# Attention and expert tail on one core: band bias by products for 32 keys in column groups over 96 stacked rows, prologue loads in another order, gathers six tiles ahead and scatters three behind

## The chip, the core and the metric

The program runs on one NeuronCore of one Trainium2 chip. A core has five engines with a queue of instructions each: TensorE (PE, with its weight loads as PEld), VectorE (DVE), ScalarE (ACT), GpSimd (POOL) and SyncE (SP, which here only issues DMAs). The metric is the device time of one execution in microseconds (us). The kernel before took 760.58 us, the median of three runs (757.05 to 767.64).

## What is computed

Two layers act on x, which is (2, 1024, 128) in f32. The attention of the first is what the change touches most.

```python
x = x + attention(layernorm(x), Wq, bq, Wk, bk, Wv, bv, rel_bias)   # 16 heads, head size 8, S = 1024
x = x + channel_mix(layernorm(x), W_r, W_k, W_v, mu_r, mu_k)        # sigmoid(.) * (relu(.)^2 @ W_v.T)
x = x + spiral_conv_block(layernorm(x), ..., w1, b1, w2, b2)        # long convolution, norm, 128 -> 512 -> 128
x = x + experts(layernorm(x), gate_w, w1, w3, w2)                   # 2048 tokens, top 2 of 8, hidden 352

# attention
scores = einsum('bqhd,bkhd->bhqk', q, k) / sqrt(8)
n = maximum(query - key, 0)          # distance; 0 for keys later than the query
bias = rel_bias[bucket(n)]           # 32 buckets: n itself below 16, logarithmic above, the last from 31 on
attn = softmax(scores + bias, axis=-1)
context = einsum('bhqk,bkhd->bqhd', attn, v)

# experts
for e in range(8):
    out = (silu(xe @ w1[e].T) * (xe @ w3[e].T)) @ w2[e].T            # only rows routed to e count
```

For a head the bias depends on query - key alone. It has one value for all keys later than the query, another for all keys 31 or more before it, and varies only between: in a tile of 128 keys, for at most 160 queries.

## The kernel before, in words

**Prologue.** Sixteen row tiles of x are normed by DVE. In four chunks of 512 tokens, PE transposes the normed rows (`transposes(c)`, L497) and projects them to q, k and v (`project(c)`, L513, L514, L516). Q and k are split into three bf16 parts each (by ACT and DVE for chunks 0 and 1, POOL takes part for chunks 2 and 3), which SP writes to DRAM (`parts_out`, L278, L280). A small table of bias values per distance goes to DRAM too, in f32 and in three bf16 parts (L266, L268).

**Pairs.** The scores are computed for 16 pairs of heads of one batch each (`Pair`). A pair's operands are loaded from DRAM into one of three sets, `set` = pair modulo 3: queries and a row of bias steps (`load_queries`, L289 and L291), keys (`load_keys`, L219) and the band tables in f32 and in bf16 parts (`load_tables`, L296 and L301). Row r of a table holds the bias values from an offset r on, and a product with a reversing matrix (FLIPB) puts the rows at the keys they belong to. A pair has 20 loads; they all count on one semaphore, `ops_in`. PE waits for the whole of it before a pair's first product. SP issues them in this order two pairs ahead, once PE has used up the last pair that had the set (`b_ready`). Pair 0's keys are loaded on ACT's queue.

**A tile.** Each pair is 16 tiles j, head a = j % 2 and key block kb = j // 2 of 128 keys. For a tile PE does, in this order: two products 128 x 512 of the transposed scores (`scores_T`, L552, into `psB`), between them two of the untransposed scores for the row maxima (`scores`, L541, into one of three `psA` banks), which belong to a tile six ahead (`AHEAD`) and thus, at the end of a pair, to the next pair; the band bias added to `psB` (`band_T`, L563: one product for each bf16 part, 128 x 160, 128 x 128 in the last key block, and in key block 3, where the band crosses a bank's border at column 512, a product for each side); and then values of an earlier tile (`values`, L580: eight products, 32 output partitions each, in four column groups, `tile_position=(0, g)`). ACT turns `psB` into probabilities (L468, L470). DVE reduces the `psA` banks to row maxima (L700, L705, L706), reduces those at the end of a pair (L712), and PE transposes them once in a pair (`max_transpose`, L591, at tile 12). They go through DRAM into rows of the next pair's queries (SP L308, L312). A product of `scores` waits for its bank to be freed by DVE (`free_bank`), one of `scores_T` for ACT's exponential two tiles before.

The scores of pair 0 and of six tiles of pair 1 come first (a loop of 22 steps at the end of the prologue, scores only), with the chunks 2 and 3 between them. POOL's queue has the splits for chunks 2 and 3, the addition of v's bias, and behind these the loads of the later layers' weights (L398).

**Tail.** The other layers run in chunks behind the attention. The experts come last: the rows are sorted by expert into 46 tiles of 128 (`TILES`). POOL gathers a tile's rows by an indirect DMA (L944) four tiles ahead into a ring of 8 (`RING_X`); PE transposes them, multiplies by w1 and w3 (L1167) and w2 (L1190); DVE puts the result into a ring of 4 (`RING_Y`, L1434), and POOL scatters it by an indirect DMA (L950) two tiles behind.

## Time and profile before

| | |
|---|---|
| median of three runs | 760.58 us (757.05 to 767.64) |
| profiled execution | 759.78 us, its span 758.0 us |
| mean granted TensorE clock | 0.907 |
| PE busy | 623.5 us (82%) |
| DVE busy | 509.1 us (67%) |
| ACT busy | 428.8 us (57%) |
| POOL busy | 164.1 us (22%) |

The span runs from the first to the last instruction of the profiled execution. Busy time is that in which an engine has an instruction in work. PE's matmuls are pipelined, so their durations overlap and a busy PE is not one at its peak. PEclk is the clock that was granted to TensorE, 1.00 for 2.4 GHz and 0.50 for 1.2 GHz. SPq is SP's own sequencer as it issues DMAs. An engine's shares are means over stages that differ: prologue up to about 75 us, pairs to 465 us, then the other layers, and the expert tiles from 589 to 745 us.

### The profile page before, as it was taken

To read this page: it belongs to the slowest core of one execution; us is meant where nothing else is said; L and a number is where in the kernel's file an instruction comes from. 1 tells how busy PE (TensorE), PEld (TensorE's weight loads), DVE (VectorE), ACT (ScalarE), POOL (GpSimd) and SP (SyncE) were. 2 spreads that over 40 slices of the span, in tenths; PEclk is the share of its full clock that TensorE was granted. 3 is DMA by queue.
4 is the path that set the end of the run, shared out by engine and by line. 5 is a ranking of instruction groups with operands and counts; after the bars stand their busy time and mean duration, and the time that the engine had idled before them with its cause. 6 is when DMAs were issued, how large, how long until landed. Compare 5 with 4: busy or idle time off the path is not lost. (4 is left out here: it accounts for less than half of the span.)

```text
span 758.0 us, 14698 instructions
## 1 busy us (share of the span) xinstructions
PE 623.5 (82%) x5140; PEld 292.4 (39%) x5140; DVE 509.1 (67%) x1627; ACT 428.8 (57%) x769; POOL 164.1 (22%) x199
## 2 busy tenths in 40 slices
...
...
DMA packets 62842, 40.17 MB, mean 53 GB/s; under 512 B 36462, under 2 KB 54759, under 8 KB 62477
## 3 DMA queue, kind: packets, MB, share of 16 engines
...
q8 instruction: 42, 0.69, 0.4%
...
q14 instruction: 30, 0.25, 0.1%
...
## 5 line engine op out<-in xcount | busy, mean ns | idle before, releaser
L468 ACT ACTIVATE sb_probs<-psB 128x128 f32<-128x128 f32 (+7 forms) x256 | 167.2, 653 | 92.2 <-PE psB L563 92.0
L700 DVE TENSOR_REDUCE sb_max_parts<-psA 128x1 f32<-128x512 f32 x256 | 176.5, 690 | 50.7 <-PE psA L541 43.0
L541 PE MATMUL psA<-sb_k_operand,sb_q_operand 53*128 53x512 bf16 x512 | 170.2, 403 | 35.2 <-DMA sb_bias_table_parts<-bias_parts 26.7
L580 PE MATMUL psV<-sb_probs,sb_v_operand 128*32 128x256 f32 x2048 | 160.7, 392 | 0.1
L552 PE MATMUL psB<-sb_q_operand,sb_k_operand 53*128 53x512 bf16 x512 | 157.1, 387 | 0.1
L470 ACT ACTIVATE sb_probs<-psB,sb_far_bias 128x896 f32<-128x896 f32 (+6 forms) x224 | 153.7, 686 | 0.0
L705 DVE TENSOR_REDUCE sb_max_parts<-psA 128x1 f32<-128x352 f32 (+1 forms) x256 | 133.0, 519 | 0.1
L563 PE MATMUL psB<-sb_bias_table_parts,sb_flip_b 128*128 128x160 bf16 (+2 forms) x864 | 98.4, 228 | 0.0
L563 PEld LDWEIGHTS psB<-sb_bias_table_parts,sb_flip_b 128*128 128x128 bf16 x864 | 50.9, 98 | 102.2 <-issue 102.2
L374 POOL COPY sb_v_operand<-sb_v_by_pair 128x64 f32<-128x64 f32 x32 | 7.2, 257 | 340.1 <-PE psB L563 328.7
L706 DVE CUSTOM_DVE_ANT_0 sb_band_scores<-psA,sb_bias_tables 128x160 f32<-128x160 f32 (+1 forms) x256 | 79.6, 311 | 0.0
L1167 PE MATMUL bank<-wt_w,context_T 128*128 x184 | 69.4, 500 | 6.5 <-DVE t_hm L1428 3.3
L552 PEld LDWEIGHTS psB<-sb_q_operand,sb_k_operand 53*128 53x128 bf16 x512 | 28.8, 94 | 99.3 <-issue 89.9
L950 POOL DMA_INDIRECT rows_y<-t_ys,t_place x46 | 46.5, 1011 | 58.7 <-DVE t_ys L1434 47.4
L541 PEld LDWEIGHTS psA<-sb_k_operand,sb_q_operand 53*128 53x128 bf16 x512 | 33.5, 94 | 64.3 <-DVE sb_max_parts L700 21.8
L1044 ACT ACTIVATE t_su<-bank 128x352 f32<-128x352 f32 x46 | 21.3, 464 | 65.2 <-PE bank L1167 40.5
L1428 DVE TENSOR_TENSOR t_hm<-t_su,bank 128x352 f32<-128x352 f32 x46 | 24.0, 521 | 47.8 <-PE bank L1167 32.0
L580 PEld LDWEIGHTS psV<-sb_probs,sb_v_operand 128*32 128x32 f32 x2048 | 42.2, 108 | 30.8 <-ACT sb_probs L468 0.6
L1048 ACT COPY context_T<-bank 128x512 f32<-128x512 f32 (+2 forms) x49 | 27.4, 558 | 44.3 <-issue 15.6
L1434 DVE COPY t_ys<-bank 128x128 f32<-128x128 f32 x46 | 13.4, 291 | 54.5 <-remote 32.2
L1190 PE MATMUL bank<-wt_w,context_T 128*128 (+1 forms) x276 | 40.1, 281 | 11.0 <-DVE t_ys L1434 10.9
L944 POOL DMA_INDIRECT t_xs<-rows_x,t_token x46 | 44.8, 973 | 13.9 <-issue 13.6
...
## 6 DMA issues: line engine op xcount, KB each, us to landing
...
```

Source lines behind the costliest of these rows:

```text
L468: ins = nc.scalar.activation(out[:, 0:edge], scores[:, 0:edge], ACT.Exp)
L470: ins = nc.scalar.activation(out[:, edge:S], scores[:, edge:S], ACT.Exp, bias=DELTA[:, bass.ds(p.n * 2 + a, 1)])
L541: nc.tensor.matmul(PA[slot % 3][:], QO[64 * a:64 * a + ROWS, p.set, 128 * qb:128 * qb + 128], KO[64 * a:64 * a + ROWS, p.set, at:at + 512] ...
L552: nc.tensor.matmul(PB[:, 1024 * a + lo:1024 * a + lo + 512], KO[64 * a:64 * a + ROWS, p.set, 128 * kb:128 * kb + 128], QO[64 * a:64 * a + ...
L563: ins = nc.tensor.matmul(PB[:, 1024 * a + c0:1024 * a + c1], FLIPB[:], TP[:, p.set, a, part, c0 - 128 * kb:c1 - 128 * kb], start=False, st ...
L580: ins = nc.tensor.matmul(PV[g:g + 32, at:at + 256], VB[:, p.set, a, kb, :], P[:, kb % KB_BUFS, a, half * 512 + at:half * 512 + at + 256], ...
L700: nc.vector.tensor_reduce(mx[:, 0:1], score_bank(t, 0)[:], AX.X, ALU.max).then_inc(s["a_used"], 1)
L705: nc.vector.tensor_reduce(mx[:, 1:2], ps[:, 0:352 + edge], AX.X, ALU.max)
L706: nc.vector.tensor_tensor_reduce(SC[:, t % 2, edge:160], ps[:, 352 + edge:512], reversed_table(p, a, edge, 160), 1.0, -3.0e38, ALU.add, AL ...
L944: pool.indirect_dma_start(XS[:, n % RING_X, :], None, XMD[h], bass.IndirectOffsetOnAxis(TOK[h][:, k:k + 1], 0)).then_inc(x_in[n % RING_X], 16)
L950: pool.indirect_dma_start(YD[h], bass.IndirectOffsetOnAxis(PLACE[h][:, k:k + 1], 0), YS[:, n % RING_Y, :], None, bounds_check=2 * S - 1, o ...
L1167: nc.tensor.matmul(out[:, 0:HID], HX[:, (n - 2) % 3, 384:512], t[w][:, bass.ds(experts[n], 1), :].rearrange("d o h -> d (o h)"), start=Tru ...
```

## The change

It has three parts.

**The band.** `band_T` treats each 32 keys of a tile apart. The three bf16 parts of the table are stacked as 3 x 32 = 96 rows, and the stationary matrix `FLIP3` (96 rows) holds the reversing 32 x 32 block three times, so that one product adds up the three parts. Group i of 32 keys needs the queries from 32 i on: 128, 96, 64 and 32 columns (64 for the last, where the band reaches into the next key block), and goes into its own column group. In key block 3 a fifth product serves the columns behind the bank's border for the last group. The table `TP` becomes 96 x 192 per head and is loaded by three DMAs for each head instead of two for both; `LOADS` becomes 24.

**The prologue.** SP issues pair 0's tables ahead of the q and k parts, the bias steps by a function of their own (`load_steps`), and the keys of head 1; ACT issues those of head 0, at its third chunk. PE takes chunk 2 ahead of the first scores, and the fourth chunk's q, k and v projections are put at three steps of the scores' loop instead of one.

**The experts.** Gathers run six tiles ahead, scatters three behind, and `RING_Y` is 5; in a step the scatter stands ahead of the gather.

```diff
     REL, SEL = sb("rel", [NB, 2 * H]), sb("sel", [NB, WCOLS])
-    FLIP, FLIPB, IDB = sb("flip", [128, 128]), sb("flip_b", [128, 128], BF16), sb("ident_b", [128, 128], BF16)
+    FLIP, FLIP3, IDB = sb("flip", [128, 128]), sb("flip_3", [96, 128], BF16), sb("ident_b", [128, 128], BF16)
     KRB = sb("key_rows_b", [5, 2 * S], BF16)
...
     QO, KO = sb("q_operand", [128, 3, S], BF16), sb("k_operand", [128, 3, 2 * S], BF16)
-    TT, TP = sb("bias_tables", [128, 3, 2, 160]), sb("bias_table_parts", [128, 3, 2, 3, 160], BF16)
+    TT, TP = sb("bias_tables", [128, 3, 2, 160]), sb("bias_table_parts", [96, 3, 2, 192], BF16)
     VB = sb("v_operand", [128, 3, 2, NBLK, 32])
...
              "b_ready exp_done pv_done evac_done max_parts max_psum max_rows max_out max_in "
-             "bq_scaled m_step own_v").split()
+             "bq_scaled m_step own_v flip_zero").split()
     s = {n: sem(n) for n in names}
...
     ops_in = [sem(f"ops_in{n}") for n in range(3)]
-    LOADS = 2 * (3 + 4 + 1) + 4
+    LOADS = 2 * (3 + 4 + 1) + 2 + 6
...
-    def load_keys(eng, p):
-
-        for a in range(2):
+    def load_keys(eng, p, heads=range(2)):
+
+        for a in heads:
             at = p.n * (16 * 3 * S) + a * DH * 3 * S
...
                                  ).then_inc(ops_in[p.set], 16)
+
+        def load_steps(p):
+            for a in range(2):
                 sp.dma_start(QO[64 * a + ROW_STEP:64 * a + ROWS, p.set, :],
...
                              ).then_inc(ops_in[p.set], 16)
-            parts = TP[:, p.set, :, :, :].rearrange("p h a c -> p (h a) c")
-            for at, seg, n in ((0, DIAG, 128), (128, EDGE, 32)):
-                sp.dma_start(parts[:, :, at:at + n], bass.AP(WPD.tensor, p.n * (2 * 3 * NPARTS) + seg,
-                                                             [[1, 128], [NPARTS, 6], [1, n]])
-                             ).then_inc(ops_in[p.set], 16)
+            for a in range(2):
+                for at, seg, n in ((0, DIAG + 96, 128), (128, DIAG + 96, 32), (160, EDGE, 32)):
+                    sp.dma_start(TP[:, p.set, a, at:at + n],
+                                 bass.AP(WPD.tensor, (p.n * 2 + a) * (3 * NPARTS) + seg, [[NPARTS, 3], [1, 32], [1, n]])
+                                 ).then_inc(ops_in[p.set], 16)
...
-        parts_out(0)
-        parts_out(1)
         sp.wait_ge(s["w_out"], 16)
         sp.wait_ge(s["wp_out"], 16)
+        load_tables(Pair(0, 0))
+        parts_out(0)
         sp.wait_ge(s["steps_out"], 16)
+        load_steps(Pair(0, 0))
+        parts_out(1)
         for c in range(2):
...
         load_queries(Pair(0, 0))
-        load_tables(Pair(0, 0))
         for c in range(2):
             sp.wait_ge(k_out[c], 32)
+        load_keys(sp, Pair(0, 0), heads=(1,))
         load_queries(Pair(0, 1))
+        load_steps(Pair(0, 1))
         load_keys(sp, Pair(0, 1))
...
                 load_queries(p + 2)
+                load_steps(p + 2)
                 load_keys(sp, p + 2)
...
         pool.memset(MHALF[:], -0.5).then_inc(s["half_ready"], 1)
+        pool.memset(FLIP3[:], 0.0).then_inc(s["flip_zero"], 1)
         pool.memset(STEPS[:, 3:5, :], 0.0).then_inc(s["steps_ready"], 1)
...
             nc.scalar.copy(XT[:, 512 * c:512 * c + 512], PV[:]).then_inc(s["xt_ready"], 1)
+            if c == 2:
+                for n in range(2):
+                    act.wait_ge(k_out[n], 32)
+                load_keys(act, Pair(0, 0), heads=(0,))
             act.wait_ge(s["bq_scaled"], 1)
...
                            V_BANKS[c].rearrange("p (n m c) -> p n m c", n=4, m=8)).then_inc(s["v_read"], 1)
-            if c == 1:
-                for n in range(2):
-                    act.wait_ge(k_out[n], 32)
-                load_keys(act, Pair(0, 0))
-
         def max_copy(p):
...
-        def project(c):
+        def project(c, what="qkv"):
             pe.wait_ge(s["xt_ready"], c + 1)
...
             xt = XT[:, 512 * c:512 * c + 512]
-            nc.tensor.matmul(Q_BANKS[c], WQ[:], xt, start=True, stop=True).then_inc(s["q_psum"], 1)
-            nc.tensor.matmul(K_BANKS[c], WK[:], xt, start=True, stop=True).then_inc(s["k_psum"], 1)
-            for n in range(4):
-                ins = nc.tensor.matmul(V_BANKS[c][:, 128 * n:128 * n + 128], xt[:, 128 * n:128 * n + 128], WV[:],
-                                       start=True, stop=True)
-            ins.then_inc(s["v_psum"], 1)
+            if "q" in what:
+                nc.tensor.matmul(Q_BANKS[c], WQ[:], xt, start=True, stop=True).then_inc(s["q_psum"], 1)
+            if "k" in what:
+                nc.tensor.matmul(K_BANKS[c], WK[:], xt, start=True, stop=True).then_inc(s["k_psum"], 1)
+            if "v" in what:
+                for n in range(4):
+                    ins = nc.tensor.matmul(V_BANKS[c][:, 128 * n:128 * n + 128], xt[:, 128 * n:128 * n + 128], WV[:],
+                                           start=True, stop=True)
+                ins.then_inc(s["v_psum"], 1)
...
         def band_T(p, j):
+
+
+
             kb, a = j // 2, j % 2
-            for half in range(2):
-                lo = half * 512
-                c0, c1 = max(lo, 128 * kb), min(lo + 512, 128 * kb + 160)
-                if c0 < c1:
-                    for part in range(3):
-                        ins = nc.tensor.matmul(PB[:, 1024 * a + c0:1024 * a + c1], FLIPB[:],
-                                               TP[:, p.set, a, part, c0 - 128 * kb:c1 - 128 * kb],
-                                               start=False, stop=part == 2)
+            edge = kb not in (3, 7)
+            for i in range(4):
+                at, n = 1024 * a + 128 * kb + 32 * i, 128 - 32 * i
+                table = TP[:, p.set, a, 0:n]
+                if i == 3 and edge:
+                    n, table = 64, TP[:, p.set, a, 128:192]
+                ins = nc.tensor.matmul(PB[32 * i:32 * i + 32, at:at + n], FLIP3[:, 96:128], table,
+                                       start=False, stop=True, tile_position=(0, 32 * i))
+            if kb == 3:
+                ins = nc.tensor.matmul(PB[:, 1024 * a + 512:1024 * a + 544], FLIP3[:], TP[:, p.set, a, 160:192],
+                                       start=False, stop=True)
             ins.then_inc(s["b_ready"], 1)
...
-        for c in range(2):
+        for c in range(3):
             transposes(c)
             project(c)
-        pe.wait_ge(s["flip_ready"], 2)
+        pe.wait_ge(s["flip_ready"], 4)
         pe.wait_ge(s["key_copies"], 32)
...
             turn, j = (Pair(0, -2), t + 16 - AHEAD) if t < AHEAD else (Pair(0, -1), t - AHEAD)
-            if t in (2, 8):
-                transposes(2 + t // 8)
-            if t in (5, 11):
-                project(2 + t // 8)
+            if t == 3:
+                transposes(3)
+            if t in (6, 8, 10):
+                project(3, "qkv"[t // 2 - 3])
             if t == AHEAD + MAX_AT:
...
         dve.wait_ge(s["flip_in"], 32)
-        nc.vector.tensor_copy(FLIPB[:], FLIP[:]).then_inc(s["flip_ready"], 1)
+        dve.wait_ge(s["flip_zero"], 1)
+        for n in range(3):
+            at = 32 * n
+            nc.vector.tensor_copy(FLIP3[at:at + 32, 96:128], FLIP[at:at + 32, 96 - at:128 - at]
+                                  ).then_inc(s["flip_ready"], 1)
         dve.wait_ge(s["w_in"], 16 * 6)
...
 TILES_FROM = START[1] + AT["gates"] + 5
-SLOTS = TILES_FROM + TILES + 4
+SLOTS = TILES_FROM + TILES + 5
 TABLE = 3 * SLOT_TILES
-RING_X, RING_Y = 8, 4
+RING_X, RING_Y = 8, 5
+GATHERED, SCATTERED = 6, 3
...
         n = slot - TILES_FROM - 2
-        return [n] if -2 <= n < TILES + 2 else []
+        return [n] if -2 <= n < TILES + 3 else []
...
             for n in tile_at_slot(slot):
+                if 0 <= n - SCATTERED < TILES:
+                    scatter(n - SCATTERED)
                 if n == -2:
-                    for m in range(3):
+                    for m in range(GATHERED - 1):
                         gather(m)
-                elif n + 4 < TILES:
-                    gather(n + 4)
-                if n >= 2:
-                    scatter(n - 2)
+                elif n + GATHERED < TILES:
+                    gather(n + GATHERED)
...
                                      ).then_inc(s[done], 1)
-            if n > -2:
+            if -2 < n <= TILES + 1:
                 pe.wait_ge(s["hx"], n + 2)
...
                 ins.then_inc(s["hx_psum"], 1)
-            if n >= 2:
+            if 2 <= n < TILES + 2:
                 y = n - 2
...
                 V.tensor_tensor(HM[:, n % 2, 0:HID], SU[:, n % 2, :], V_PS[:, 0:HID], ALU.mult).then_inc(s["hm"], 1)
-            if n >= 2:
+            if 2 <= n < TILES + 2:
                 y = n - 2
```

PE's queue in a middle tile of a pair, before. L552 is `scores_T`, L541 `scores`, L563 the band, L580 the values.

```order
L552 MATMUL psB<-sb_q_operand,sb_k_operand 128x512
L541 MATMUL psA<-sb_k_operand,sb_q_operand 128x512
L552 MATMUL psB<-sb_q_operand,sb_k_operand 128x512
L541 MATMUL psA<-sb_k_operand,sb_q_operand 128x512
L563 MATMUL psB<-sb_bias_table_parts,sb_flip_b 128x160 x3
L580 MATMUL psV<-sb_probs,sb_v_operand 32x256 x4
```

The same place after the change. L562 is `scores_T`, L551 `scores`, L577 the band, L596 the values.

```order
L562 MATMUL psB<-sb_q_operand,sb_k_operand 128x512
L551 MATMUL psA<-sb_k_operand,sb_q_operand 128x512
L562 MATMUL psB<-sb_q_operand,sb_k_operand 128x512
L551 MATMUL psA<-sb_k_operand,sb_q_operand 128x512
L577 MATMUL psB<-sb_bias_table_parts,sb_flip 32x128
L577 MATMUL psB<-sb_bias_table_parts,sb_flip 32x96
L577 MATMUL psB<-sb_bias_table_parts,sb_flip 32x64 x2
L596 MATMUL psV<-sb_probs,sb_v_operand 32x256 x4
```

Only the band's rows differ; its four products stand between the scores and the values, which have 32 output partitions as well.

PE's queue in the prologue, behind the second chunk, before. L497 are transposes, L513, L514 and L516 the projections to q, k and v.

```order
L541 MATMUL psA<-sb_k_operand,sb_q_operand 128x512 x4
L497 MATMUL psV<-sb_ident,xn 128x128 x4
L541 MATMUL psA<-sb_k_operand,sb_q_operand 128x512 x6
L513 MATMUL psB<-xn_T,sb_wq 128x512
L514 MATMUL psB<-xn_T,sb_wk 128x512
L516 MATMUL psB<-sb_wv,xn_T 128x128 x4
L541 MATMUL psA<-sb_k_operand,sb_q_operand 128x512 x6
L497 MATMUL psV<-sb_ident,xn 128x128 x4
L541 MATMUL psA<-sb_k_operand,sb_q_operand 128x512 x6
L513 MATMUL psB<-xn_T,sb_wq 128x512
L514 MATMUL psB<-xn_T,sb_wk 128x512
L516 MATMUL psB<-sb_wv,xn_T 128x128 x4
```

After the change (L504 transposes; L521, L523, L526 the projections):

```order
L504 MATMUL psV<-sb_ident,xn 128x128 x4
L521 MATMUL psB<-xn_T,sb_wq 128x512
L523 MATMUL psB<-xn_T,sb_wk 128x512
L526 MATMUL psB<-sb_wv,xn_T 128x128 x4
L551 MATMUL psA<-sb_k_operand,sb_q_operand 128x512 x6
L504 MATMUL psV<-sb_ident,xn 128x128 x4
L551 MATMUL psA<-sb_k_operand,sb_q_operand 128x512 x6
L521 MATMUL psB<-xn_T,sb_wq 128x512
L551 MATMUL psA<-sb_k_operand,sb_q_operand 128x512 x4
L523 MATMUL psB<-xn_T,sb_wk 128x512
L551 MATMUL psA<-sb_k_operand,sb_q_operand 128x512 x4
L526 MATMUL psB<-sb_wv,xn_T 128x128 x4
```

The third chunk stands ahead of all scores, the fourth is in three pieces with scores between them.

SP's queue where it has written the steps, up to the second chunk's parts, before:

```order
L270 DMA step_rows<-sb_steps 32x5120
L278 DMA q_parts<-sb_q_split 128x512
L280 DMA q_parts<-sb_q_split 128x2x512
L278 DMA k_parts<-sb_k_split 128x512
L280 DMA k_parts<-sb_k_split 128x2x512
```

After the change:

```order
L270 DMA step_rows<-sb_steps 32x5120
L299 DMA sb_bias_tables<-bias_vectors 128x2x128
L299 DMA sb_bias_tables<-bias_vectors 128x2x32
L304 DMA sb_bias_table_parts<-bias_parts 96x1x128
L304 DMA sb_bias_table_parts<-bias_parts 96x1x32 x2
L304 DMA sb_bias_table_parts<-bias_parts 96x1x128
L304 DMA sb_bias_table_parts<-bias_parts 96x1x32 x2
L278 DMA q_parts<-sb_q_split 128x512
L280 DMA q_parts<-sb_q_split 128x2x512
```

Pair 0's tables, which stood behind its queries, are now issued first, and by eight DMAs instead of four.

## Rows read from the trace of the kernel before

**Rows 1.** The page's costliest groups: line, engine, tiles | busy us, mean ns | idle before

```profile
L580 PE MATMUL psV<-sb_probs,sb_v_operand 128*32 128x256 f32 x2048 | 160.7, 392 | 0.1
```

**Rows 2.** Three windows of 20 us: busy time per engine, then PEclk, DMA share

```profile
60.00:80.00 20.00, 15.38 (x45) 3.33 (x44) 19.72 (x57) 3.11 (x7) 19.86 (x28) 0.52 0.30 67
...
240.00:260.00 20.00, 19.90 (x211) 6.74 (x208) 18.94 (x58) 16.09 (x28) 0.41 (x2) 1.00 0.18 40
...
440.00:460.00 20.00, 20.00 (x195) 6.75 (x197) 0.00 (x0) 16.50 (x28) 0.00 (x0) 1.00 0.02 5
```

**Rows 3.** Timeline, one tile on PE: start us, us, engine, line, tiles

```profile
251.28 0.39 PE L552 MATMUL psB<-sb_q_operand,sb_k_operand 53*128 53x512 bf16 x1
...
251.81 0.34 PE L563 MATMUL psB<-sb_bias_table_parts,sb_flip_b 128*128 128x128 bf16 x3
...
252.08 0.64 PE L580 MATMUL psV<-sb_probs,sb_v_operand 128*32 128x256 f32 x8
...
252.66 0.39 PE L552 MATMUL psB<-sb_q_operand,sb_k_operand 53*128 53x512 bf16 x1
```

**Rows 4.** Timeline, the maxima's product on PE, behind the values of a tile

```profile
271.01 0.64 PE L580 MATMUL psV<-sb_probs,sb_v_operand 128*32 128x256 f32 x8
...
271.47 0.22 PE L591 MATMUL psA<-sb_ident_b,sb_max_high_low 128*32 128x128 bf16 x1
...
271.62 0.39 PE L552 MATMUL psB<-sb_q_operand,sb_k_operand 53*128 53x512 bf16 x1
```

**Rows 5.** Timeline, DVE, at the change from one pair to the next

```profile
245.36 0.20 DVE L712 TENSOR_REDUCE sb_row_max<-sb_max_parts 128x16 f32<-128x48 f32 x1
...
268.68 0.20 DVE L712 TENSOR_REDUCE sb_row_max<-sb_max_parts 128x16 f32<-128x48 f32 x1
...
269.64 0.68 DVE L700 TENSOR_REDUCE sb_max_parts<-psA 128x1 f32<-128x512 f32 x1
...
270.91 0.69 DVE L700 TENSOR_REDUCE sb_max_parts<-psA 128x1 f32<-128x512 f32 x1
```

**Rows 6.** Timeline, the prologue: norms, last load, first scores, projection, DVE's wait

```profile
24.49 2.14 DVE L657 TENSOR_SCALAR xn<-x,sb_ln_mv,sb_ln_rstd 128x128 f32<-128x128 f32 x8
...
30.59 1.06 SPq L301 DMA_DIRECT2D sb_bias_table_parts<-bias_parts  x2
...
35.16 1.01 PE L541 MATMUL psA<-sb_k_operand,sb_q_operand 53*128 53x512 bf16 x3 [13.94 <-DMA sb_bias_table_parts<-bias_parts]
...
41.38 2.08 PE L513 MATMUL psB<-xn_T,sb_wq 128*128 128x512 f32 x2
...
47.44 0.69 DVE L700 TENSOR_REDUCE sb_max_parts<-psA 128x1 f32<-128x512 f32 x1 [4.71 <-PE psA L541]
```

**Rows 7.** Timeline, weight loads on POOL, pair 2's table load, its first product

```profile
67.80 0.79 POOL L398 DMA_DIRECT2D wt_r<-in_W_r  x1
...
84.41 13.09 SPq L301 DMA_DIRECT2D sb_bias_table_parts<-bias_parts  x2
...
103.28 0.61 PE L541 MATMUL psA<-sb_k_operand,sb_q_operand 53*128 53x512 bf16 x1 [12.77 <-DMA sb_bias_table_parts<-bias_parts]
```

**Rows 8.** Timeline, SP's queue, first and last load of one pair's operands

```profile
253.56 1.81 SPq L289 DMA_DIRECT2D sb_q_operand<-q_parts  x3
...
261.64 1.06 SPq L301 DMA_DIRECT2D sb_bias_table_parts<-bias_parts  x2
```

**Rows 9.** Timeline, the expert stage: two tiles on PE and on POOL

```profile
649.57 1.45 PE L1167 MATMUL bank<-wt_w,context_T 128*128 x4 [0.27 <-issue]
...
651.96 1.35 PE L1167 MATMUL bank<-wt_w,context_T 128*128 x4
...
650.25 0.98 POOL L944 DMA_INDIRECT t_xs<-rows_x,t_token  x1 [0.30 <-issue]
...
652.85 0.97 POOL L944 DMA_INDIRECT t_xs<-rows_x,t_token  x1 [0.30 <-issue]
```

**Rows 10.** Waits of the whole span: who for whom, us in total, times, longest

```profile
DVE t_ys L1434 <- remote: 32.2, 9, 3.8
```

## The prediction, made before the changed kernel ran

> **What bounds the kernel now.** I read the page first, then the busy time by windows, then the timeline of one tile, one change of pairs, the prologue and the expert stage, and last the waits. The attention covers about 75 to 465 us of the 758 us. In its middle PE is busy 19.9 of 20 us, DVE 18.9 and ACT 16.1, at clock 1.00; behind 440 us, where DVE has nothing left, PE is at 20.00 of 20 [rows 2]. So PE sets the pace, and DVE stands close behind. How close is seen in two places. A tile takes PE 1.38 us with a 128-column band (about 1.42 with 160 columns): 0.53 for the score products, 0.27 for the three band products, 0.58 for the values [rows 3]. DVE, where it has a backlog, needs 1.27 us for the same tile, and 0.96 us between pairs for the row maximum [rows 5]. A pair takes 23.3 us now [rows 5]; DVE's own floor is 16 x 1.27 + 1.0 = 21.3.
>
> Before that lie two long waits for operand loads: 13.9 us ahead of the first scores [rows 6], and 12.8 us at 90.5 us, where PE waits for pair 2's operands while the expert weights fill the DMA engines [rows 7]. Two projections inside the first pair's scores also starve DVE, one of them for 4.71 us [rows 6].
>
> **The band products.** Three products with 128 output partitions become four with 32 each, in four column groups, over 96 rows instead of 128; two tiles in 16 get a fifth. Do column groups run at once? The values say so: 8 products of a mean of 392 ns [rows 1] are done in 0.64 us [rows 3]. A second thing can be read there. Behind a tile's values, the score product starts 0.58 us after they began [rows 3], but the maxima's product, which also has 32 columns, starts 0.46 us after [rows 4]. A change of shape thus costs about 0.1 us, and none is paid between two 32-column shapes. The new band has the values' shape, so one of three changes per tile goes as well. Band and change fall from 0.27 (0.31 at 160 columns) to about 0.06: PE's tile becomes 0.53 + 0.06 + 0.58 = 1.17 us.
>
> The bounds: if the four products ran one behind another and the change stayed, the phase would be 352/384 of the present one, since their widths sum to 128 + 96 + 64 + 64 columns against 384 in [rows 3]: 0.25 us, and a tile 1.36. Below, nothing can take more than the whole 0.31. I take 1.17, by [rows 3, 4]. For short products the Trainium skill (TensorEngine Tiling (Array Packing), Instruction Overhead) says that each matmul carries some 60 cycles whatever its width. Four of these would be 0.1 us instead of 0.06 and the last tiles of the stage would cost 1 us more; the middle would not change, since DVE sets it either way.
>
> At 1.17 PE passes DVE, and a pair takes DVE's 21.3, not 16 x 1.17. I add 0.3 for the tile with two pieces of values and the tile in which ACT also copies the context out: 21.6, a gain of 1.7 us. DVE works on 14 pairs behind the wait at 103 us: **-24 us** (-12 with a tile of 1.36, -28 at the bare floor). The ten tiles ahead of that wait gain 0.14 each: **-1.4**. Behind DVE's last pair some 22 tiles remain; there PE's 1.17 and ACT's 16.5 of 20 us [rows 2], which is 1.17 of 1.42, are level. With 1.20 per tile: **-4.8** (-1 to -5.5).
>
> **The operand loads.** The band tables now are 6 DMAs per pair instead of 2: four more on SP's queue, and nothing is taken off it. Two issues take 1.06 us [rows 8], so about 2.1 us is added to a queue that is busy for 9.1 us from the start of a pair (253.56 to 262.70). DVE turns to that pair at 269.64 [rows 5], 16.1 us after the first issue, and the product has to be there 0.6 earlier: 15.5. The ten tiles between shrink by 1.4. The margin from last issue to need thus goes from 6.4 to 2.9 us. The flight of the last load is at most 31.65 to 35.16 = 3.5 us, as the prologue shows with 1536 small pieces under way [rows 6]. The new tables have 576 pieces (96 rows, three segments, two heads), so I take the flight below 2.9 and the cost as **0**; up to 0.6 us for 13 pairs, 8 us, is in the range.
>
> **The prologue.** Pair 0's tables are issued ahead of the q and k parts, one head's keys move from ACT's queue to SP's, and behind the q parts SP has ten issues left instead of twelve. The last issue comes at about 31.2 instead of 31.65, with 16 rows in place of 1536 pieces; the load should be there at 33. Into the wait goes the third projection block. Its norms are done by 26.6 [rows 6]; transposes, copy and three projections of about 2 us each (L513 takes 2.08 at the half clock [rows 6]) end at about 33.4. The scores start there: **-1.6** (0 to -3). DVE's 4.71 us for this block goes. The fourth block is cut in three, each of 2 us less the 0.7 us of scores that stand ready; that about equals what it costs in one piece: together **-4.9** (-2 to -7).
>
> **The wait for pair 2.** The weight loads start at 67.80, and the wait ends at 103.28, 35.5 us later; SP's two table issues alone were held up 13.09 us [rows 7]. In the new order the weights start about 13 us earlier, at 55 (the fourth block's keys are ready earlier, and POOL's split and addition follow). 960 of the 1536 pieces that came last are gone, for which I take 3 us. Pair 2's operands would be there at 55 + 32.5 = 87.5. PE reaches them 15.3 us after pair 0's start, now 90.5, then about 90.5 - 1.6 - 4.9 - 1.4 = 82.6. The wait shrinks to 5: **-7.5** (0 to -12.8).
>
> **The expert stage.** Gathers run six tiles ahead instead of four, scatters three behind instead of two, with a ring of five. PE's short tile is 2.39 us, POOL's pair of transfers 2.60 [rows 9], yet the stage averages about 3.2. Its long waits are DVE's on something that the profile calls remote, nine times, up to 3.8 us [rows 10]. Nothing there names a late gather or scatter, so I only count the few late gathers: **-3**. If the remote waits come from the two-deep scatters, POOL's 2.60 is the new pace, 0.6 x 37 tiles = -22; if deeper gathers crowd POOL, +5.
>
> **The sum.** -24 - 1.4 - 4.8 + 0 - 1.6 - 4.9 - 7.5 - 3 = -47. The profiled execution took 759.8, which gives 712.6; the median shown is 0.8 above it: **713 us**.
>
> **The rivals.** First, the column groups don't overlap and PE stays the bound at 1.36: the middle gains 12 instead of 24, the end 1 instead of 4.8: 713 + 12 + 4 = 729. Against it stand [rows 4]; for it, that no row shows 96-row products there. Chance 0.15. Second, the operands land later than I take it, and the wait for pair 2 stays: 713 + 8 + 7.5 = 729. Chance 0.13. Third, the remote waits go: 713 - 19 = 694, chance 0.10. Fourth, the change leaves the path alone, because PE's records only look full: within 2%, about 750; [rows 2] speak against it, 0.04.
>
> The one on the other side is TensorE's clock. Once DVE sets the pace, PE stops for a moment in every tile. That is the state of 60 to 80 us, where DVE is busy 19.7 of 20 and the granted clock is 0.52, nearly its 1.2 GHz level [rows 2]. At that level a tile of 1.17 takes 2.34. It decides from 3.4 us of loss per pair, which eats the 47 us over 14 pairs: three or four tiles of each 16 at the low level. If half of them were, 8 x 1.07 = 8.6 us per pair would be added: 713 + 120 = 833. Against it: a slow PE is the bound again, and so gets no pauses; and in the stretch of 60 to 80 PE did a third of the work per tile. Chance 0.05. The Trainium skill (TensorE: Matmul & The Clock Gate, A second HAM failure mode) describes such a case, where small pauses between groups of products let the clock swing between its two levels.
>
> **How the numbers follow.** My forecast, 704 to 722, has 0.53. The range for 8 in 10 takes in the first two rivals and half of the third: 699 to 734. A measurement of this kernel can tell some 2% from no change, which is 745 to 776. Faster by more: 0.53 + 0.15 + 0.13 + 0.10, less a little for sums of bad ends, 0.89; same 0.06; slower 0.05.
>
> **What would show it.** Right: band products in one burst under 0.3 us with the values right behind; DVE without gaps at 1.27 us per tile, pairs of 21.3 to 21.9; PE's score products released by DVE; the first wait about 12 us with projections in it, the second about 5. Wrong: pairs above 22.5; a wait of every pair's first product for a table DMA; a clock below 1.00 between 110 and 420 us; expert tiles off 3.2 us.

## The result: faster by 4.8%, 13 us above the forecast

| | before | changed |
|---|---|---|
| median | 759.74 us of 4 runs (757.05 to 767.64) | 726.11 us of 4 runs (721.22 to 730.41) |
| ratio | | 0.9518 (0.9466 to 0.957) |
| profiled execution | 759.78, span 758.0 | 725.86, span 724.0 |

The forecast was 713 with a range of 699 to 734. The page of the changed kernel begins:

```profile
span 724.0 us, 15152 instructions
## 1 busy us (share of the span) xinstructions
PE 585.4 (81%) x5332; PEld 267.5 (37%) x5332; DVE 497.6 (69%) x1629; ACT 426.8 (59%) x769; POOL 164.5 (23%) x200
```

The same windows as [rows 2], the last one moved to where DVE's work ends (busy time of each engine, then granted clock, DMA share, GB/s):

```profile
60.00:80.00 20.00, 13.19 (x39) 2.55 (x38) 15.59 (x50) 2.00 (x5) 17.16 (x29) 0.50 0.57 188
240.00:260.00 20.00, 18.69 (x237) 5.77 (x239) 19.42 (x63) 16.75 (x29) 0.41 (x2) 1.00 0.19 46
400.00:420.00 20.00, 19.48 (x245) 5.46 (x237) 3.77 (x14) 19.07 (x34) 0.00 (x0) 1.00 0.03 6
```

In the middle PE no longer fills its time and DVE does; behind DVE's last pair PE and ACT are level. One tile on PE and the change of pairs on DVE, the counterparts of [rows 3] and [rows 5]:

```profile
162.78 0.39 PE L562 MATMUL psB<-sb_q_operand,sb_k_operand 53*128 53x512 bf16 x1
...
163.32 0.23 PE L577 MATMUL psB<-sb_bias_table_parts,sb_flip 96*32 96x128 bf16 x4
163.37 0.62 PE L596 MATMUL psV<-sb_probs,sb_v_operand 128*32 128x256 f32 x8
163.92 0.39 PE L562 MATMUL psB<-sb_q_operand,sb_k_operand 53*128 53x512 bf16 x1
```

```profile
143.24 0.20 DVE L732 TENSOR_REDUCE sb_row_max<-sb_max_parts 128x16 f32<-128x48 f32 x1
...
164.75 0.20 DVE L732 TENSOR_REDUCE sb_row_max<-sb_max_parts 128x16 f32<-128x48 f32 x1
...
165.36 0.68 DVE L720 TENSOR_REDUCE sb_max_parts<-psA 128x1 f32<-128x512 f32 x1
```

The four band products last 0.23 us together, and the values follow 0.05 us behind their start. A tile takes PE 1.14 us where nothing holds it, against 1.38 to 1.42. A pair takes 21.51 us (164.75 less 143.24) against 23.32.

Where the 34.0 us of span went, read from the first score reduction on DVE of each pair (for the last pair also that of its last tile, where the tiles behind DVE's last begin) and the last product of the transposed scores:

| stretch | before | changed | difference | forecast |
|---|---|---|---|---|
| start to DVE's pair 0 | 35.85 | 39.08 | +3.2 | -1.6 |
| pair 0's scores | 32.16 | 26.29 | -5.9 | -4.9 |
| pair 1's, with the wait for pair 2 | 35.99 | 34.03 | -2.0 | -8.9 |
| 14 pairs on DVE | 327.3 | 302.5 | -24.8 | -24 |
| the tiles behind DVE's last | 30.8 | 25.7 | -5.1 | -4.8 |
| tail | 295.9 | 296.4 | +0.5 | -3 |

The middle came as forecast. The prologue gave 4.7 where 15.4 was expected. Its rows, first SP's and the first scores, then POOL's weights, SP's tables of pair 2 and PE's two waits (start, duration, then in brackets the idle time before and what ended it):

```profile
20.19 4.42 SPq L304 DMA_DIRECT2D sb_bias_table_parts<-bias_parts  x6
...
30.45 3.72 SPq L289 DMA_DIRECT2D sb_q_operand<-q_parts  x6
...
34.27 1.34 SPq L219 DMA_DIRECT2D sb_k_operand<-k_parts  x4
...
38.39 1.01 PE L551 MATMUL psA<-sb_k_operand,sb_q_operand 53*128 53x512 bf16 x3 [4.96 <-DMA sb_k_operand<-k_parts]
...
61.41 0.79 POOL L406 DMA_DIRECT2D wt_r<-in_W_r  x1
...
76.93 0.58 PE L562 MATMUL psB<-sb_q_operand,sb_k_operand 53*128 53x512 bf16 x1 [4.86 <-DMA sb_q_operand<-row_maxima]
...
81.34 15.88 SPq L304 DMA_DIRECT2D sb_bias_table_parts<-bias_parts  x6
...
98.69 0.61 PE L551 MATMUL psA<-sb_k_operand,sb_q_operand 53*128 53x512 bf16 x1 [6.43 <-DMA sb_bias_table_parts<-bias_parts]
```

The last key load of pair 0 is issued by 35.61 (34.27 + 1.34), and PE starts 2.8 us later. Not all of the +3.2 belongs to the change. PE's first transposes, before and changed, already lie 1.3 us apart, since DVE's second norm waited 1.65 us for x instead of 0.34, and nothing of the change stands ahead of that load:

```profile
10.35 1.12 PE L497 MATMUL psV<-sb_ident,xn 128*128 128x128 f32 x4 [2.14 <-DVE xn L657]
```

```profile
11.69 1.12 PE L504 MATMUL psV<-sb_ident,xn 128*128 128x128 f32 x4 [3.19 <-DVE xn L673]
```

This start varies from 10.4 to 12.1 us over the profiles below. From the first transposes to the first scores it is 24.8 us before and 26.7 changed (26.7 to 27.0 in all eight profiles with this order and these loads on SP): +1.9 us is the change's. The wait for pair 2's tables shrank from 12.77 [rows 7] to 6.43, but a new one of 4.86 stands ahead of it, for pair 0's maxima, whose small transfers lie among the weights.

### The profile page after: what moved, and what is told of

It reads as the page before. It is cut to its first block and busy times, and to the rows that moved or that the text cites. A ratio compares the mean times of both kernels' runs of the same rounds, so it can differ in the third digit from the quotient of the medians.

```text
span 724.0 us, 15152 instructions
## 1 busy us (share of the span) xinstructions
PE 585.4 (81%) x5332; PEld 267.5 (37%) x5332; DVE 497.6 (69%) x1629; ACT 426.8 (59%) x769; POOL 164.5 (23%) x200
## 5 line engine op out<-in xcount | busy, mean ns | idle before, releaser
L551 PE MATMUL psA<-sb_k_operand,sb_q_operand 53*128 53x512 bf16 x512 | 181.4, 411 | 26.2 <-DMA sb_bias_table_parts<-bias_parts 11.4
L562 PE MATMUL psB<-sb_q_operand,sb_k_operand 53*128 53x512 bf16 x512 | 161.1, 389 | 7.1 <-DMA sb_q_operand<-row_maxima 6.0
L596 PE MATMUL psV<-sb_probs,sb_v_operand 128*32 128x256 f32 x2048 | 157.7, 387 | 0.3 <-ACT sb_probs L475 0.3
L562 PEld LDWEIGHTS psB<-sb_q_operand,sb_k_operand 53*128 53x128 bf16 x512 | 31.5, 94 | 105.8 <-issue 51.1
L551 PEld LDWEIGHTS psA<-sb_k_operand,sb_q_operand 53*128 53x128 bf16 x512 | 39.6, 94 | 82.4 <-DVE sb_max_parts L720 41.8
L577 PE MATMUL psB<-sb_bias_table_parts,sb_flip 96*32 96x64 bf16 (+3 forms) x1024 | 59.3, 214 | 0.0
L577 PEld LDWEIGHTS psB<-sb_bias_table_parts,sb_flip 96*32 96x32 bf16 x1024 | 26.3, 93 | 87.9 <-issue 87.9
L1065 ACT ACTIVATE t_su<-bank 128x352 f32<-128x352 f32 x46 | 21.4, 466 | 62.7 <-PE bank L1188 38.4
L596 PEld LDWEIGHTS psV<-sb_probs,sb_v_operand 128*32 128x32 f32 x2048 | 44.5, 110 | 5.0 <-ACT sb_probs L475 0.8
```

The source lines that it names most:

```text
L551: nc.tensor.matmul(PA[slot % 3][:], QO[64 * a:64 * a + ROWS, p.set, 128 * qb:128 * qb + 128], KO[64 * a:64 * a + ROWS, p.set, at:at + 512] ...
L562: nc.tensor.matmul(PB[:, 1024 * a + lo:1024 * a + lo + 512], KO[64 * a:64 * a + ROWS, p.set, 128 * kb:128 * kb + 128], QO[64 * a:64 * a + ...
L577: ins = nc.tensor.matmul(PB[32 * i:32 * i + 32, at:at + n], FLIP3[:, 96:128], table, start=False, stop=True, tile_position=(0, 32 * i))
L596: ins = nc.tensor.matmul(PV[g:g + 32, at:at + 256], VB[:, p.set, a, kb, :], P[:, kb % KB_BUFS, a, half * 512 + at:half * 512 + at + 256], ...
```

## The experiments

The column "before" is the median of the kernel before on the same chip, and the ratio is against it. The kernel before itself took 738 to 765 us, by the chip, so the ratios are compared, and stretches of the profiles. Three more kernels leave something out and were run once each, beside a kernel before of 761.89 or 764.96; they stand in the text.

| kernel | median | before | ratio (interval) | last scores product at |
|---|---|---|---|---|
| changed | 726.11 | 759.74 | 0.9518 (0.9466 to 0.957) | 427.6 |
| tables on POOL | 723.54 | 761.89 | 0.9498 (0.9451 to 0.9545) | 425.1 |
| weights spread | 715.08 | 761.89 | 0.9404 (0.9342 to 0.9465) | 416.6 |
| prologue undone | 735.56 | 761.89 | 0.9691 (0.9622 to 0.9761) | 436.8 |
| both | 711.30 | 764.96 | 0.9329 (0.925 to 0.9407) | 412.2 |
| experts undone, scatter first | 739.55 | 764.96 | 0.9682 (0.9594 to 0.9769) | 430.7 |
| experts as before | 704.43 | 744.17 | 0.9476 (0.9428 to 0.9525) | 428.2 |
| gather first | 695.07 | 744.17 | 0.9345 (0.9293 to 0.9396) | 428.5 |
| band only | 716.30 | 744.17 | 0.9646 (0.9596 to 0.9695) | 436.8 |
| best | 681.27 | 738.41 | 0.9214 (0.9165 to 0.9263) | 414.0 |

### Who sets a pair: DVE's first reduction reads a quarter

```diff
-nc.vector.tensor_reduce(mx[:, 0:1], score_bank(t, 0)[:], AX.X, ALU.max)
+nc.vector.tensor_reduce(mx[:, 0:1], score_bank(t, 0)[:, 0:128], AX.X, ALU.max)
```

> The first reduction of each tile on DVE reads 128 of its 512 columns (0.69 us becomes about 0.28), so three quarters of the keys of that half are left out of the row maxima; everything else as changed. Theory A (DVE sets the pair time): pairs fall from 21.52 to the next bound, which is PE with 16 tiles of 1.13 to 1.39 us and its hiccups, or SP's issues, 19 to 20.5 us; 14 pairs give 14 to 35 us, about 700 us in all. Rival B (SP's load loop sets it: 14.0 us to the first product): the pair is 14.0 plus six tiles of 1.13, 20.8 us, and each first product waits for its table load by over 0.5 us. Rival C (PE or ACT sets it): pairs stay at 21.3 to 21.5.

One run: 718.26 us. Change of pairs on DVE, a pair's first product on PE, and two windows:

```profile
140.20 0.20 DVE L732 TENSOR_REDUCE sb_row_max<-sb_max_parts 128x16 f32<-128x48 f32 x1
160.81 0.20 DVE L732 TENSOR_REDUCE sb_row_max<-sb_max_parts 128x16 f32<-128x48 f32 x1
```

```profile
161.57 0.39 PE L551 MATMUL psA<-sb_k_operand,sb_q_operand 53*128 53x512 bf16 x1 [0.76 <-DMA sb_bias_table_parts<-bias_parts]
...
204.11 0.39 PE L551 MATMUL psA<-sb_k_operand,sb_q_operand 53*128 53x512 bf16 x1 [2.10 <-DMA sb_bias_table_parts<-bias_parts]
```

```profile
140.00:160.00 20.00, 18.72 (x255) 5.43 (x258) 16.53 (x66) 17.93 (x32) 0.41 (x2) 1.00 0.20 49
...
204.00:208.00 4.00, 3.89 (x34) 0.96 (x36) 2.11 (x8) 2.00 (x4) 0.00 (x0) 0.57 0.06 11
```

With DVE at 16.5 of 20 us a pair falls from 21.51 to 20.61, and no further: now every first product waits for its tables. So DVE sets the pair in the changed kernel, and the table loads, which come last on SP's queue, stand 0.9 us behind it. That is both theories at once, A for the kernel as it is and B for the next step. The gain in total, 7.8 us, is less than A's low end, since B's bound was so near and some pairs took 21.9 to 22.9. One of those is in the rows: PE stood still for 2.10 us ahead of 204.11, and from 204 to 208 the granted clock is 0.57, near the 1.2 GHz level; from 208 on it is back at 1.00.

### The tables issued by POOL

```diff
-                load_tables(p + 2)                    # SP
+                load_tables(pool, p + 2)              # POOL, behind values(p + 1)
```

Pair 0's and 1's tables stand in POOL's queue where it waits in the prologue, pair 2's ahead of the weights; they count on semaphores of their own.

> All eight table loads of a pair are issued on POOL's queue instead of SP's, in the prologue too; everything else as changed. Theory A (DVE sets the pair time of 21.52 us; the six-fold issues on SP only cost where they run late): SP's issues of a pair fall from 12.5 to about 7.2 us, the small waits of a pair's first product for a table load vanish, the two long pairs (21.89 and 22.79) become 21.5, and the other pairs stay at 21.4 to 21.5; in the prologue the first scores come at about 34 instead of 38.4. In total 3 to 6 us less than the changed kernel: 720 to 723. Rival B (the loop of SP's queue sets the pair time: 14.0 us from a pair's first issue to its first product and 7.5 to the next issue): pairs fall below 21.1, and the total to 712 or less. Rival C (the order of SP's prologue costs nothing, the first scores wait for the third projection block): they stay at 38.

Median 723.54, ratio 0.9498: inside the changed kernel's interval. SP's issues of a pair, first in the changed kernel and then here, and the one long wait that PE has here:

```profile
129.00 3.71 SPq L289 DMA_DIRECT2D sb_q_operand<-q_parts  x6
...
136.18 0.90 SPq L299 DMA_DIRECT2D sb_bias_tables<-bias_vectors  x2
137.12 4.38 SPq L304 DMA_DIRECT2D sb_bias_table_parts<-bias_parts  x6
```

```profile
149.57 3.65 SPq L301 DMA_DIRECT2D sb_q_operand<-q_parts  x6
...
153.98 2.70 SPq L220 DMA_DIRECT2D sb_k_operand<-k_parts  x8
```

```profile
105.09 0.60 PE L566 MATMUL psB<-sb_q_operand,sb_k_operand 53*128 53x512 bf16 x1 [10.81 <-DMA sb_q_operand<-row_maxima]
```

SP's issues fall from 12.5 us to 7.1, and pairs stay at 21.52: B has fallen. The long pairs of the changed kernel (21.89, 22.79) are gone, which with two smaller ones is worth 1.5 us. The first scores come at 36.4, 2.0 earlier, not 4.4; and 1.3 of the 2.0 is the earlier arrival of x. From the first transposes to the first scores it is 25.95 us instead of 26.71. PE waits for the key load there, so C's reason is wrong, but its size (nothing) is nearer than A's: the keys still wait behind six query loads. Pair 2's scores begin 12 us earlier, at 86.7, and then PE waits 10.8 us for pair 1's maxima. The wait has moved, not gone: it belongs to whatever small transfer comes while the weights are under way.

### The weights in pieces

```diff
-        for dst, src in later_loads:
-            pool.dma_start(dst, src).then_inc(loaded, 16)
...
+            if 1 <= p.n <= 12:
+                for dst, src in later_loads[p.n - 1::12]:
+                    pool.dma_start(dst, src).then_inc(loaded, 16)
```

w1 and w3 are cut by expert, w2 by two experts.

> The loads of the later layers' weights are cut into pieces of one or two experts and issued by POOL in pairs 1 to 12, four a pair, instead of in one go at 61 us; everything else as changed. Theory A (the weight traffic makes both remaining waits of the prologue, 4.86 us for pair 0's maxima and 6.43 us for pair 2's tables): both vanish, pair 2's first product comes at about 87 instead of 98.7, and the pairs behind stay at 21.5: 11 us less, about 715. Rival B (the loads are late through SP's own queue, 5.4 us of table issues): the waits shrink by less than half, 721 or more. Rival C (the traffic is only moved: each pair's own loads, which land 1.5 us ahead of need, now come late by the pieces' time): pairs of 22.0 and more, no gain in total, 724 to 728.

Median 715.08, ratio 0.9404. Pair 2's first product, and that of pair 11:

```profile
86.95 0.39 PE L551 MATMUL psA<-sb_k_operand,sb_q_operand 53*128 53x512 bf16 x1
```

```profile
282.27 0.39 PE L551 MATMUL psA<-sb_k_operand,sb_q_operand 53*128 53x512 bf16 x1 [0.87 <-DMA sb_bias_table_parts<-bias_parts]
```

Both waits are gone, as A has it: 86.95 without a wait, at the full clock. Of the 11.7 us against the changed kernel 0.9 is the earlier arrival of x. The edit cuts the loads and also spreads them over twelve pairs; which of the two does it was not separated. C is there too but small: four pairs take 22.2 to 22.6 (the next expectation says six), 3 us in all more than at 21.52. That the pieces delay their loads is likely, not shown: the changed kernel has long pairs too.

### Both

> Weights spread over pairs 1 to 12 and all table loads on POOL's queue. Theory A (DVE sets the pairs, the two prologue waits are the weights' and the long pairs come from SP's late issues): first scores at 36.4, pair 0's maxima without a wait, pair 2's first product at 86, every pair 21.5 without the 22.2 to 22.6 that six pairs show with the weights spread alone: 3 to 5 us less than its 715, 710 to 712. Rival B (the pieces sit ahead of the tables in POOL's queue and make them late): pairs of 22.5 and more, 716 or above.

Median 711.30, ratio 0.9329, as A has it. Pair 2 starts at 85.0, and all pairs but two take 21.52 (21.8 and 22.1).

### The prologue's order undone

The order on SP, PE and ACT is that of before; band and expert stage are the changed ones.

```diff
-        for c in range(3):
+        for c in range(2):
             transposes(c)
...
-            if t == 3:
-                transposes(3)
-            if t in (6, 8, 10):
-                project(3, "qkv"[t // 2 - 3])
+            if t in (2, 8):
+                transposes(2 + t // 8)
+            if t in (5, 11):
+                project(2 + t // 8)
```

> The changed kernel with the prologue's order of before on PE, SP and ACT (third and fourth projection blocks in the scores' loop, tables behind the queries, pair 0's keys on ACT), with the new band and the new expert stage. Theory A (the new order cost 3.2 us at the first scores and gave 5.9 back in the projections, and the rest was lost in the wait for the weights): the first scores come at about 38 (35.2 plus 2 to 3 for four more table issues), pair 0's scores take 32 us instead of 26, and pair 2's first product comes at 103 to 106 instead of 98.7: 4 to 7 us more than the changed kernel, 730 to 733. Rival B (the order is worth nothing): 726 within 2.

Median 735.56, ratio 0.9691. First scores 38.2, pair 0's scores 31.6 us, pair 2's first product 106.5, the last scores product 9.2 us later than in the changed kernel: A, a little above its range. Undoing the order brings the first scores no earlier than 38.2 (26.5 us behind the first transposes), since the four more table issues then stand ahead of them in their old place. So the +1.9 at the start comes with the band's part, not with the new order; the kernel with the band alone, below, has the same 26.7. How much of it is the issues themselves is open: with all tables on POOL only 0.8 came back.

### The band alone, and without its products

Band only: prologue and expert stage as before.

> Only the band's part of the change (products for 32 keys in column groups, 96 stacked rows, six table loads a pair), with the prologue's order and the expert stage of before. Theory A (the band alone gives the 23 us of 13 pairs, about 2 us at the first pair, and 5 in the last 22 tiles, and the four more issues of SP cost 3 us at the first scores): the last band product at 436, which is 26 earlier than before, and 732 to 737 in all. Rival B (the band and the new prologue only work together): a gain below 20 us, over 740.

Ratio 0.9646; 716.30 us against 744.17 on that chip, and 25.3 us earlier than before at the last scores product (436.8 against 462.1, the latter from a profile on which the kernel before took 759.78). A's times for the whole were meant for a chip on which the kernel before takes 760. On the same chip the kernel with the new prologue as well (experts as before) takes 704.43: the prologue adds 11.9, of which the profiles show 8.6 by the last scores product.

```diff
-                band_T(p, j)
+                # b_ready comes from the second product of scores_T
```

> The band products are left out (the bias of near keys is missing); the second product of the transposed scores releases ACT in their place. Looked at where DVE has nothing left, some 20 tiles ahead of the last band, in which PE's tile is 1.13 us with the band and was 1.38 to 1.42 before. Theory A (the four products run at once and cost 0.05 to 0.06, and their change of shape is shared with the values): PE's tile falls by at most 0.06, to 1.07 to 1.10, or is set by ACT's 1.13 to 1.17 and does not fall at all; pairs in the middle stay at 21.4 to 21.5. Rival B (the products still cost 0.15 to 0.2 a tile): 0.95 in tiles where ACT doesn't hold PE, and pairs fall by over 1 us.

One run: 720.6 us. One tile behind DVE's last pair, without the band and (second fence) in the changed kernel:

```profile
402.90 0.60 PE L562 MATMUL psB<-sb_q_operand,sb_k_operand 53*128 53x512 bf16 x2
...
403.43 0.64 PE L598 MATMUL psV<-sb_probs,sb_v_operand 128*32 128x256 f32 x8
```

```profile
405.87 0.60 PE L562 MATMUL psB<-sb_q_operand,sb_k_operand 53*128 53x512 bf16 x2
...
406.41 0.23 PE L577 MATMUL psB<-sb_bias_table_parts,sb_flip 96*32 96x128 bf16 x4
...
406.45 0.62 PE L596 MATMUL psV<-sb_probs,sb_v_operand 128*32 128x256 f32 x8
```

The values start 0.53 us after the tile's start without the band and 0.58 with it: the four products cost 0.05. Tiles take 1.10 there and 1.13 in the changed kernel, but ACT is busy nearly all the time in both (17.74 of 18 us and 19.07 of 20), so the 0.05 is read on PE alone. Pairs take 21.29 instead of 21.52. B has fallen.

The fifth product of key block 3 is another matter. It has 128 output partitions, not 32:

```profile
416.69 0.60 PE L562 MATMUL psB<-sb_q_operand,sb_k_operand 53*128 53x512 bf16 x2
...
417.38 0.19 PE L580 MATMUL psB<-sb_bias_table_parts,sb_flip 96*128 96x32 bf16 x1
417.50 0.64 PE L596 MATMUL psV<-sb_probs,sb_v_operand 128*32 128x256 f32 x8
```

There the values start 0.81 us after the tile's start, so this one product of 32 columns costs 0.23, over four times as much as the other four together, and its tiles take 1.39 us instead of 1.13. The prediction put it at nothing. It stands between 32-partition products and so adds changes of shape, which agrees with the 0.1 us for each that the prediction read from [rows 3, 4], though no run changes its shape alone. In the middle it is hidden behind DVE.

### The expert stage

Only eight tiles gathered:

```diff
-                elif n + GATHERED < TILES:
+                elif n + GATHERED < RING_X:
```

> In the expert stage only the first 8 tiles are gathered, and the others work on what lies in the ring, so that POOL issues one indirect DMA for a tile instead of two (1.3 us instead of 2.6). Theory A (the pauses of 5 us at every third tile come from POOL's pace of 2.60 us and its back-to-back issues): the stage falls from 3.30 us a tile to 2.3 to 2.5, 36 to 45 us less in all, about 685. Rival B (the pauses come from something else, the scatters' ring or PE's own loads): 3.2 to 3.3 a tile, 722 to 728.

One run: 696.75 us, and 2.61 us a tile: far from B's 3.2, but above A's 2.3 to 2.5. The scatter ahead of the gather, as in the change, with the old depths:

```diff
-RING_X, RING_Y = 8, 5
-GATHERED, SCATTERED = 6, 3
+RING_X, RING_Y = 8, 4
+GATHERED, SCATTERED = 4, 2
```

> The changed kernel with gathers four tiles ahead, scatters two behind and a ring of four, as before; the scatter still stands ahead of the gather. Theory A (the deeper rings are worth nothing, since POOL's 2.60 us and the pauses set the pace): 3.28 to 3.35 us a tile, the total within 2 us of the changed kernel's 726. Rival B (they gave 3 us): 729.

Median 739.55, 3.45 us a tile: neither theory, the depths are worth more than both say. The ratio of 0.9682 lies clear of the changed kernel's. PE now waits for gathers, 24 times, where the changed kernel does so twice (3.3 us):

```profile
PE bank L1201 <- DMA t_xs<-rows_x,t_token: 19.1, 24, 2.2
```

Then the stage wholly as before, and the change's depths with the gather first:

> The changed kernel with the expert stage wholly as before: gather ahead of scatter in a step, gathers four tiles ahead, scatters two behind, a ring of four. Theory A (the stage's change is worth about nothing as a whole: POOL's 2.60 us a tile sets the pace either way): 3.30 to 3.36 us a tile, the total 724 to 730. Rival B (the change of the stage gave what its depth costs when it is undone with the scatter left first, 3.45 against 3.30 us a tile): 3.4 or more, 733 and above.

> The changed kernel with gathers six tiles ahead, scatters three behind and the ring of five, but the gather ahead of the scatter in a step. Theory A (only POOL's sum of 2.60 us counts, the order inside a step does not once there is depth): 3.28 to 3.34 us a tile, total 724 to 729. Rival B (the scatter first is what keeps the ring turning): over 3.4 a tile.

Times from the first to the last tile's first product, over 45 (the depths are tiles that gathers run ahead, tiles that scatters run behind, and `RING_Y`):

| kernel | depths, first in a step | kernel before took | us a tile |
|---|---|---|---|
| before | 4/2/4, gather | 759.74 | 3.33 |
| changed | 6/3/5, scatter | 759.74 | 3.30 |
| experts undone | 4/2/4, scatter | 764.96 | 3.45 |
| gathers left out | 6/3/5, scatter | 764.96 | 2.61 |
| experts as before | 4/2/4, gather | 744.17 | 2.82 |
| gather first | 6/3/5, gather | 744.17 | 2.58 |
| best | 6/3/5, gather | 738.41 | 2.59 |

A window of 20 us in the stage: changed, gathers left out, experts as before, gather first.

```profile
600.00:620.00 20.00, 15.54 (x81) 11.48 (x80) 4.67 (x12) 5.62 (x12) 12.23 (x13) 0.91 0.21 36
```

```profile
600.00:620.00 20.00, 20.00 (x125) 15.83 (x124) 7.06 (x18) 9.16 (x18) 8.70 (x9) 1.00 0.08 26
```

```profile
600.00:620.00 20.00, 18.80 (x104) 13.96 (x103) 5.98 (x15) 7.59 (x16) 15.43 (x16) 1.00 0.24 48
```

```profile
600.00:620.00 20.00, 20.00 (x126) 15.94 (x125) 7.16 (x18) 9.29 (x18) 15.43 (x16) 1.00 0.25 48
```

Without the gathers, PE's work fills its time at 2.29 us a tile and the pauses at every third tile are gone. So they hang on POOL's transfers, as A has it. With the gather first, PE is full too, although POOL's pair takes 2.60 us: PE gains 0.3 us a tile on POOL out of the lead that the depths give, 27 tiles long, until a gap of 7.1 us in which POOL catches up (6.5 without the gathers: the gap has another cause). With the old depths the lead is used up sooner: 2.82. There the change's depth is worth 0.24 x 45 = 10.8 us in the stage, and 9.4 between the medians (704.43 and 695.07).

In the profiles of the kernel before and the changed one this gain does not show: 3.33 and 3.30. Both have, nine times, the wait of [rows 10]:

```profile
DVE t_ys L1455 <- remote: 30.4, 9, 3.8
```

One of the nine on PE, and then DVE, in the changed kernel:

```profile
601.25 0.83 PE L1211 MATMUL bank<-wt_w,context_T 128*128 x6
```

```profile
605.33 0.29 DVE L1455 COPY t_ys<-bank 128x128 f32<-128x128 f32 x1 [3.74 <-remote]
```

PE's products have ended by 602.1, and the DVE copy that waits for them starts 3.2 us later (2.0 to 3.3 in all nine). ACT has such waits too, up to 5.1 us.

Six more profiles with the change's expert stage, beside kernels before of 762 and 765 us, have the wait 9 to 12 times; their stages take 3.20 to 3.33. So the 0.03 between before and changed is less than the spread of one and the same code. None of the four kernels run where the kernel before takes 738 to 744 has the wait. Nor have two on a chip with a kernel before of 765: the one without gathers, and the one with the old depths and the scatter first, which is the slowest of all. So the wait is not the whole of a slow stage.

The same stage as before takes 3.33 on one chip and 2.82 on another (2.84 in the kernel with the band alone), 23 us between them, about all of what those chips are faster. Whether the order inside a step matters was not separated with the new depths: the scatter-first order was never run on such a chip, nor the gather-first with the new depths on one of the others. With the old depths it can be seen beside kernels before of 760 and 765: gather first 3.33 with 3 waits of PE for a gather, scatter first 3.45 with 24; the two differ in the rest of the kernel as well. The expectations of the stage as before and of the gather first meet neither theory, since both come from runs on the slower chip. What holds back the releases in the pauses stays open.

### A version that beats both

Weights spread, tables on POOL, and the gather ahead of the scatter.

> Weights spread over pairs 1 to 12, all table loads on POOL's queue, and in the expert stage the gather ahead of the scatter with the new depths (six, three, ring of five). The last kernels were compared with a kernel before that took 744.17 us, the earlier ones with one of 761.89 or 764.96, so their expert stages (2.58 us a tile with the gather first, 3.30 with the scatter first) may differ by the chip. Theory A (the order inside a step decides): 2.6 us a tile whatever the kernel before takes; 696 to 700 if that takes about 762, 678 to 684 if it takes about 744. Rival B (the chip decides, the order does nothing): beside a kernel before of about 762 the stage stays at 3.2 to 3.3 and the total at 709 to 713. Up to the last band product both expect 412 to 413.

Median 681.27, ratio 0.9214 (0.9165 to 0.9263): 57 us less than the kernel before on the same chip. The kernel before took 738.41 there, so the question of order and chip could not be told apart. Its pairs take 21.52 but for one of 21.82. The kernel with both load changes alone has 0.9329 (0.925 to 0.9407); the two intervals only just touch.

## Why the prediction was right, and where it was off

The sum was -47 and the profiled executions differ by 33.9. The step that carried it, the pace of the pairs, was right in mechanism and size: PE's tile 1.17 forecast and 1.14 measured, DVE at its floor, a pair 21.6 forecast and 21.51 measured, 14 pairs -24 and -24.8, the last tiles -4.8 and -5.1. The first rival (products one behind another) is out by 0.05 us for four. By the Trainium skill (TensorEngine Tiling (Array Packing), Instruction Overhead) my estimate for them was 0.1, from some 60 cycles each; the trace has half, so here that overhead was not paid four times in a row. The fifth product in two tiles of each 16 was put at nothing and took 0.23 each.

**The wait for pair 2** is the step that failed: "the weights start about 13 us earlier, at 55", "Pair 2's operands would be there at 55 + 32.5 = 87.5". They started at 61.41 and the tables were there at 98.7. 6.4 of the 11.2 us are the start. POOL's last split of the fourth block ended at 57.0, and its addition took 4.5 us more. Most of that delay is inherited: the block's projections stand in the loop of the first scores, and that began at 38.4, not at the 33.5 of the forecast, 4.9 later. That its keys are projected two steps behind its queries cost POOL only 0.8:

```profile
53.94 1.16 POOL L396 TENSOR_TENSOR sb_k_full<-sb_k_full,sb_k_split 128x512 f32<-128x512 f32 x1 [0.82 <-ACT sb_k_split L448]
```

The other 4.8 are the flight: 37.3 us instead of 32.5. I took 3 us off for fewer pieces, yet the six issues took 15.88 us among the weights where two had taken 13.09 [rows 7]. And I had one transfer in view where any would do: the maxima of pair 0, which PE now reached sooner, waited for 4.86. Spreading the weights shows the size of the whole: 11.7 us at pair 2's first product (98.7 to 87.0), 0.9 of it x's arrival. The forecast has a slip of its own, too: 87.5 less 82.6 leaves 4.9 of the 12.8 us, which is 7.9 less and not 7.5.

**The ten tiles ahead of that wait** were to gain 1.4 and gained 0.3: 14.9 us from their start to the last product ahead of the wait, instead of 15.3. PE had had less to do before them (busy for 13.2 of the 20 us from 60 to 80, 15.4 in the kernel before), and the clock stood at 0.50 over the first 10 us of them, where in the kernel before it was 1.00 from 82 on:

```profile
76.00:86.00 10.00, 8.86 (x68) 2.48 (x72) 7.75 (x24) 6.51 (x12) 1.16 (x3) 0.50 1.00 266
```

**The first scores**: "the last issue comes at about 31.2". It came at 35.6. 1.3 us of the 4.4 is the late x, which no forecast could hold. Six table issues took 4.42 us, 0.73 each, where I had 0.53 from [rows 8], and they stood ahead of the q parts, which everything behind waits for; the second key load stood behind six query loads as well. Undone, the start was no better (38.2), so what was mis-sized came with the band's part: 1.9 us more than before, where -1.6 was forecast.

**The operand loads of the pairs**: the cost of 0 was nearly right, 1.5 us, but the margin was not. I had 2.9 us left; the issues took 3.3 us more than before instead of 2.1, and the tables land as they are needed. The second rival was thus close: half of it (the wait for pair 2 stays) came true in part, and in the other half the loads were 0.9 us a pair from setting the pace.

**The expert stage** was put at -3 and gave 1.5 in the stage, less than the same code varies by, with 2 us lost elsewhere in the tail. The third rival (the remote waits go) did not come in this run and did on other chips; the pace that I gave it, POOL's 2.60, is not a floor, since the lead lets PE run at 2.29 for 27 of the 46 tiles.

**The clock** stayed at 1.00 from 120 to 420 us, and its rival did not come. Its mechanism is real in small: with DVE lightened, one stop of 2.10 us was followed by 4 us at 0.57. The longest stop of the changed kernel between 120 and 400 us, 1.83, had no such effect:

```profile
360.35 0.39 PE L551 MATMUL psA<-sb_k_operand,sb_q_operand 53*128 53x512 bf16 x1 [1.83 <-DMA sb_bias_table_parts<-bias_parts]
```

```profile
360.00:364.00 4.00, 3.39 (x44) 1.21 (x48) 3.16 (x9) 2.44 (x5) 0.00 (x0) 1.00 0.09 18
```

But the length of a stop doesn't decide it. With the weights spread, a shorter one was followed by some 3.4 us at the low level:

```profile
348.30 0.39 PE L551 MATMUL psA<-sb_k_operand,sb_q_operand 53*128 53x512 bf16 x1 [1.31 <-DMA sb_bias_table_parts<-bias_parts]
```

```profile
348.00:352.00 4.00, 3.70 (x34) 0.87 (x36) 2.86 (x9) 2.04 (x4) 0.00 (x0) 0.62 0.09 18
```

Over all profiles, seven first products that came 1.3 to 2.3 us late went with such a stretch, and five that came 1.5 to 2.3 us late (2.26 in the kernel with the expert stage as before) did not. What decides between them stays open.

The Trainium skill (TensorE: Matmul & The Clock Gate, A second HAM failure mode) has small pauses between groups of products as enough for a swing of the clock; in the changed kernel the pauses of every tile, with PE busy for 288 of the 300 us from 120 to 420, did not do it.
